# A turned context kept in device memory by the first stage that makes it and read back by three later ones

## The chip, the cores and the metric

The kernel runs on one core of one Trainium2 chip. The metric is device time of one execution in microseconds (us), lower is better. The profiler records one execution; its timeline gives the order of things, starting at 0 at the span's start.

## What is computed

A decoder of four layers works on 1024 rows of 128 numbers, `x`. A second input, the context `ctx_1024`, has 6404 rows of 128 numbers, and four of the twelve sublayers read it. Cut to those lines:

```python
# L0_xattn: a 3x3 kernel per head is made out of a projection of the whole context
x = x + _L0_xattn_ref(_layernorm(x), ctx_1024, ..., mask_SxS_bc0)
# L1_xattn and L2_xattn: 16 heads of 8 numbers, keys and values of the context
x = x + _L1_xattn_ref(_layernorm(x), ctx_1024, ctx_1024, mask_BxSxS2_if1, Wq, Wk, Wv, Wo, bo)
x = x + _L2_xattn_ref(_layernorm(x), ctx_1024, mask_BxS2_bk0, q_w, q_b, kv_w, kv_b, proj_w, proj_b)
# L3_xattn: keys and values at sampled positions between rows of the context
x = x + _L3_xattn_ref(ctx_1024, ctx_1024, _layernorm(x), mask_BxS2_if0, Wk, bk, Wv, bv, ...)
```

Each of them begins with a product of the context and weights (K = ctx Wk, V = ctx Wv, or the projection by hist_W of L0_xattn). None of them changes the context.

## The kernel before

P is 128, the context is KT = 51 tiles of 128 rows (6404 rows, padded to SP = 6528), and `k.ps` is PSUM with 8 banks of 512 numbers. TensorE sums over the partition dimension, so a product with the context needs it turned: channels on the partitions, rows of the context along the free dimension. That is the tile `ctxT`, 128 x 6528 floats.

A sublayer is a sequence of stages. A stage is a block in which each engine has its own program; semaphores order the engines within the block, and at the block's end all engines meet (in the trace this is line L68). So nothing of the next block begins before the last engine of this one is done. Within a block the order of the work on each engine is the order in which it is written; there is no planner.

`context_turned` (L1109) makes `ctxT` in a block of its own. SP loads the context by rows in four transfers (L1127, L1129), TensorE turns the 51 tiles by a product with the identity matrix (L1143), VectorE copies 13 banks of PSUM to `ctxT` (L1151). It is called four times:

- in `context_kernels` (L2512, sublayer L0_xattn). The block behind it projects `ctxT` by `hist_w` (L2565); ScalarE squares the result (L2592); meanwhile SP issues the 24 loads of `qstack` and `kstack` that the function `load_stacks` holds (passed in as `beside`, L2891). Those are used only by a much later block.
- in `masked_attention` (L1864, L1_xattn) and in `cross_attention` (L1948, L2_xattn), both times ahead of `context_sides` (L1178), the key stage. There 13 groups of 4 tiles go through a key product (L1217) and value products (L1221). ScalarE reads the key product (L1244, L1246), VectorE and GpSimd split it into three bfloat16 parts (L1264, L1271, L1297, L1299), SP stores the parts (L1311) and in three portions the values (L1319). The parts lie in three buffers: from the fourth group on, ScalarE waits for the store of three groups ago.
- in `deformable_lines` (L3952, the last sublayers), after a block that loads two bias rows (`load`, L262) and ahead of a block that copies `ctxT` to `ctxz`, two columns further right and with zeros around it (L3972 to L3977). The last block of the function makes the table of keys and values: for each tile two products (L3999), VectorE adds the bias (L4012), SP stores 256 KB (L4018), with three buffers again. At the same time ScalarE's queue issues 33 loads, of weights and small vectors, for the layers behind (L3987 to L3991).

## Time and profile before

| | us |
|---|---|
| median of 3 runs | 5533.56 |
| lowest, highest run | 5533.49, 5537.25 |
| the profiled execution, its own time | 5538.99 |
| its span in the trace | 5537.2 |

The profile's page gives busy time per engine, the span in 40 slices, the DMA queues, the chain of work that ended last, and groups of instructions by line with what ended the idle time before them. The page itself is one long average over very different stages; the stages that this change touches take some 350 us of the span, and they are read from the timeline (instructions in order of time, merged) and from windows (busy time and DMA in a stretch). Engines: PE is TensorE, PEld its weight loads, DVE VectorE, ACT ScalarE, POOL GpSimd, SP SyncE; SPq and ACTq are the DMA issues of SP and ACT. DMA queue q1 is SP's, q10 is ACT's.

### The profile page before, as it was taken

The page shows a single profiled execution, that of the slowest core. Times are in us where ns is not written, and L with a number is a line of the kernel's source. Part 1 is how long each engine was busy: PE and PEld are TensorE (multiplying, and loading weights), DVE is VectorE, ACT ScalarE, POOL GpSimd, SP SyncE. Part 2 cuts the span into 40 slices and gives each one's busy share as a digit, 9 for nine tenths or more (in the row PEclk, how much of TensorE's full clock was granted, in tenths as well). Part 3 has the DMA queues.
Part 4 walks back from the last instruction along what each step waited for, and adds up shares of the span by engine and source line. Part 5 has one row for each costly group of instructions (what it writes and reads, how often), then busy time and mean ns, then how long its engine had stood idle before and what let it go on. Part 6 is the DMA issues. An engine that isn't in the chain of part 4 may idle for free. (4 is left out here: it accounts for less than half of the span.)

```text
span 5537.2 us, 98710 instructions
## 1 busy us (share of the span) xinstructions
PE 4106.1 (74%) x37632; PEld 1563.3 (28%) x37668; DVE 3561.2 (64%) x9663; ACT 2637.9 (48%) x3507; POOL 776.1 (14%) x990
## 2 busy tenths in 40 slices
PE   4956999954799999999865999999978675601114
PEld 2333444432222222222342222222225443300002
DVE  5544666576888888888246888888843566631213
ACT  2522566651266666666413888888861011100001
POOL 0000000002000000000003000000000004777772
PEclk9967999976699999999876999999989887855567
DMA  0020000052301112111005111111110400000000
GB/s 14 1 63 16 12 12 12 5 205 76 121 22 33 33 29 82 27 28 29 8 4 166 30 43 43 45 40 40 41 17 25 154 0 8 14 13 13 13 13 8
DMA packets 144189, 216.02 MB, mean 39 GB/s; under 512 B 52385, under 2 KB 106509, under 8 KB 141971
## 3 DMA queue, kind: packets, MB, share of 16 engines
q1 hardware_dynamic: 102106, 191.29, 12.6%
q0 software_dynamic: 20480, 10.53, 1.3%
q10 hardware_dynamic: 21128, 7.88, 0.6%
q8 instruction: 298, 4.88, 0.4%
q14 instruction: 177, 1.44, 0.1%
HBM read 160.66 MB, written 48.94 MB: 38 GB/s over the span
## 5 line engine op out<-in xcount | busy, mean ns | idle before, releaser
L1764 ACT ACTIVATE probs<-ps 128x1024 f32<-128x1024 f32 x1632 | 1593.0, 1024 | 441.1 <-PE ps L1704 435.9
L1819 DVE CUSTOM_DVE_ANT_0 junk<-ps,mask 128x512 bf16<-128x512 f32 (+1 forms) x1664 | 1039.3, 668 | 125.2 <-PE ps L1658 87.2
L1720 PE MATMUL ps<-probs,vstack 128*18 128x512 f32 x6528 | 875.6, 600 | 0.0
L1658 PE MATMUL ps<-kturned,qturned 49*64 49x512 bf16 (+3 forms) x5178 | 791.0, 391 | 56.7 <-DVE maxima L1819 21.7
L1819 DVE CUSTOM_DVE_ANT_0 junk<-ps,nothing 128x512 bf16<-128x512 f32 (+1 forms) x1080 | 670.2, 657 | 131.9 <-PE ps L1658 131.5
L3464 POOL DMA_INDIRECT line<-table,index x640 | 621.1, 970 | 678.1 <-DVE index L3837 483.2
L1704 PE MATMUL ps<-qturned,kturned 53*64 53x512 bf16 x6528 | 625.8, 394 | 21.1 <-ACT probs L1764 13.6
L1658 PEld LDWEIGHTS ps<-kturned,qturned 49*64 49x64 bf16 (+1 forms) x5178 | 216.9, 103 | 876.3 <-issue 412.1
L3591 PE MATMUL ps<-ident,attended 128*128 128x128 f32 x8 | 3.8, 475 | 515.1 <-DVE attended L3861 515.1
L1689 PE MATMUL ps<-maskT,split 64*128 64x512 bf16 x1632 | 320.8, 384 | 2.6 <-DVE maxima L1819 2.5
L1704 PEld LDWEIGHTS ps<-qturned,kturned 53*64 53x64 bf16 x6528 | 186.5, 104 | 413.3 <-issue 253.6
L3844 DVE TENSOR_TENSOR prod<-line,frac 128x1280 f32<-128x1280 f32 x8 | 11.9, 1492 | 410.5 <-DMA line<-table,index 410.4
L3021 PE MATMUL ps<-plane,bands 32*32 32x512 f32 x6720 | 250.5, 610 | 25.6 <-DVE top L3176 25.6
L3120 ACT COPY powerT<-ps 128x512 f32<-128x512 f32 x280 | 164.2, 586 | 188.7 <-PE ps L3035 188.7
L1290 POOL MEMSET vall<- 128x408 f32 x4 | 3.1, 861 | 1777.9 <-POOLq L68 1777.9
L3675 ACT ACTIVATE score<-score 128x80 f32<-128x80 f32 x8 | 2.2, 269 | 518.0 <-DVE score L3854 518.0
L1819 DVE DVE_READ_ACCUMULATOR2_ANT maxima<- 128x1 f32 x2744 | 228.5, 83 | 0.0
L1815 DVE CUSTOM_DVE_ANT_0 junk<-ps,twins 128x512 bf16<-128x512 f32 x292 | 197.4, 688 | 42.1 <-PE ps L1658 32.0
L3112 ACT ACTIVATE power<-power,bias 128x512 f32<-128x512 f32 x280 | 202.0, 725 | 44.0 <-DVE bias L3184 44.0
L3166 DVE SCALAR_TENSOR_TENSOR plane<-keep,ps 128x1024 f32<-128x1024 uint8 x144 | 175.7, 1220 | 65.5 <-PE ps L3003 65.1
L3176 DVE CUSTOM_DVE_ANT_0 power<-ps,lose 128x512 f32<-128x512 f32 x280 | 176.9, 688 | 42.6 <-PE ps L3021 42.6
L1774 ACT ACTIVATE twins<-ps 128x512 f32<-128x512 f32 x292 | 171.3, 598 | 51.5 <-PE ps L1658 48.3
(736 smaller groups left out, 5342.1 us busy)
## 6 DMA issues: line engine op xcount, KB each, us to landing
vstack<-values_heads SPq DMA_DIRECT2D x128, 229.5 KB, 4.7
mask_raw<-in_mask_BxSxS_if SPq DMA_DIRECT2D x8, 3202.0 KB, 18.4
kturned<-keys_parts SPq DMA_DIRECT2D x384, 54.0 KB
kturned<-keys_parts SPq DMA_DIRECT2D x384, 48.0 KB
table<-lines SPq DMA_DIRECT2D x51, 256.0 KB, 3.4
line<-table,index POOLq DMA_INDIRECT x640, 2.3
keys_parts<-parts SPq DMA_DIRECT2D x24, 384.0 KB, 2.7
kapart<-keys_apart SPq DMA_DIRECT2D x160, 48.0 KB
```

The lines of the kernel that those rows point to most:

```text
L1658: last = nc.tensor.matmul(ring(e)[part, 0:hi - lo], qturned[rows, h % 3, m * P + part.start:m * P + part.stop], src, start=True, stop=True ...
L1689: nc.tensor.matmul(k.ps[:, 2 * (u % 2) + first, :], k.split[mine, :], maskT[mine, t, :], start=True, stop=False, skip_group_check=True)
L1704: last = nc.tensor.matmul(k.ps[to, 2 * (u % 2) + first, :], kturned[rows, h % 2, t * P + 64 * first:t * P + 64 * first + 64], qturned[rows ...
L1720: last = nc.tensor.matmul(k.ps[at:at + PAIR, 4, :], vstack[:, h % 2, first, t, :], probs[:, (h * KT + t) % slots, first, :], start=(t < 2) ...
L1764: nc.scalar.activation(probs[:, u % slots].rearrange("p b n -> p (b n)"), k.ps[:, bank:bank + 2, :].rearrange("p b n -> p (b n)"), ACT.Exp ...
L1815: nc.vector.tensor_tensor_reduce(junk[:, bank_of[e], :], ring(e), twins[:, twin[apart] % TWINS, :], 1.0, -3.0e38, ALU.add, ALU.max, maxima ...
L1819: nc.vector.tensor_tensor_reduce(junk[:, bank_of[e], 0:hi - lo], ring(e)[:, 0:hi - lo], lost, 1.0, -3.0e38, ALU.subtract, ALU.max, maxima[ ...
L3021: last = nc.tensor.matmul(k.ps[32 * j:32 * j + 32, i, :], bands[32 * i:32 * i + 32, 4 * g + j, c, :], plane[32 * i:32 * i + 32, u % 2, j, ...
L3112: nc.scalar.activation(part, part, ACT.Exp, bias=bias[:, u % 2, 1, i:i + 1], scale=1.0 / TINY).then_inc(powers, 1)
L3166: nc.vector.scalar_tensor_tensor(out=plane[:, u % 2, 2 * pair:2 * pair + 2, b * BANK + 1:(b + 1) * BANK + 1], in0=mid(keep[:, win % 2, b * ...
L3176: nc.vector.tensor_tensor_reduce(power[:, u % 2, i, b * BANK:(b + 1) * BANK], k.ps[:, i, :], lose[:, win % 2, i, b * BANK:(b + 1) * BANK], ...
L3464: nc.gpsimd.indirect_dma_start(line[:, t % 4, j, :], None, lines_of, bass.IndirectOffsetOnAxis(ap=index[:, t, j:j + 1], axis=0)).then_inc( ...
```

## The change

`context_turned` is called once, in `context_kernels`. SP stores `ctxT` to a new tensor in device memory, `k.turned_dram` (128 x 6528 floats, 3264 KB), at the start of the block behind it, ahead of the 24 loads, and waits for the store at the block's end. Both key stages begin with seven loads on ScalarE's queue, of 8 tiles each (the last of 3), and TensorE waits for a load before every second group. In `deformable_lines` three blocks fall away (the bias loads, the turning, the copy); the last block loads the bias rows and, in four pieces (4, 12, 16 and 19 tiles), the context straight into `ctxz`, ahead of those 33 loads on the same queue, and does the small fills and copies on VectorE first.

```diff
@@ context_sides
+        context_loaded = [s.sem(f"context_loaded{i}") for i in range(0, len(groups), 2)]
...
             for g, ts in enumerate(groups):
                 n = len(ts) * P
+                if g % 2 == 0:
+                    pe.wait_ge(context_loaded[g // 2], 16)
...
+            for i in range(0, len(groups), 2):
+                lo, hi = groups[i][0] * P, min((groups[i][0] + 8) * P, SP)
+                act.dma_start(ctxT[:, lo:hi], k.turned_dram[:, lo:hi]).then_inc(context_loaded[i // 2], 16)
             for g, ts in enumerate(groups):
                 n = len(ts) * P
                 act.wait_ge(key_product, g + 1)
@@ masked_attention, and the same in cross_attention
-            ctxT = context_turned(k, g)
+            ctxT = g.sb("ctxT", [P, SP])
@@ context_kernels
             ctxT = context_turned(k, g)
+            turned_stored = g.sem("turned_stored")
...
             def _(sp):
+                sp.dma_start(k.turned_dram, ctxT[:]).then_inc(turned_stored, 16)
                 beside(sp)
+                sp.wait_ge(turned_stored, 16)
@@ deformable_lines
-        load(k, [(bias[:, 0, :], row(k, n + "bk", D)), (bias[:, 1, :], row(k, n + "bv", D))])
         with Stage(nc) as f:
-            ctxT = context_turned(k, f)
-            with Stage(nc) as e:
-                done = e.sem("done")
-                block = e.block()
-
-                @block.vector
-                def _(dve):
-                    nc.vector.memset(ctxz[:, 0:2], 0.0).then_inc(done, 1)
...
-                    nc.vector.tensor_copy(ctxz[:, 2:S + 2], ctxT[:, 0:S]).then_inc(done, 1)
-        with Stage(nc) as f:
+            cuts = [0, 4 * P, 16 * P, 32 * P, S]
...
             def _(act):
                 with nc.allow_non_contiguous_dma("a few small vectors lie by partition"):
+                    act.dma_start(bias[:, 0, :], row(k, n + "bk", D)).then_inc(bias_loaded, 16)
+                    act.dma_start(bias[:, 1, :], row(k, n + "bv", D)).then_inc(bias_loaded, 16)
+                    for i in range(len(cuts) - 1):
+                        act.dma_start(ctxz[:, 2 + cuts[i]:2 + cuts[i + 1]], k.turned_dram[:, cuts[i]:cuts[i + 1]]).then_inc(context_loaded[i], 16)
                     act.dma_start(*first_mask).then_inc(loaded, 16)
...
             def _(pe):
+                pe.wait_ge(edges_ready, 5)
                 for t in range(KT):
+                    for i in range(len(cuts) - 1):
+                        if t * P == cuts[i]:
+                            pe.wait_ge(context_loaded[i], 16)
...
+                nc.vector.memset(ctxz[:, 0:2], 0.0).then_inc(edges_ready, 1)
...
+                dve.wait_ge(bias_loaded, 32)
                 for t in range(KT):
...
+                sp.wait_ge(edges_ready, 5)
@@ build
+        k.turned_dram = nc.dram_tensor("context_turned", (P, SP), F32, kind="Internal").ap()
```

How the instructions stand in a row, at the two places where queues change. SP in sublayer L0_xattn, from the context loads to the block's end (L68), of the kernel before:

```order
 L1127 DMA rows<-in_ctx 4x128
 L1129 DMA rows<-in_ctx 128x16x128 x2
 L1129 DMA rows<-in_ctx 128x18x128
 L68 UNCONDITIONAL_BRANCH
 L2554 UNCONDITIONAL_BRANCH
 L2891 DMA qstack<-parts 8x8x1152 x12
 L2891 DMA kstack<-parts 8x8x1024 x12
 L68 UNCONDITIONAL_BRANCH
```

and of the changed one:

```order
 L1127 DMA rows<-in_ctx 4x128
 L1129 DMA rows<-in_ctx 128x16x128 x2
 L1129 DMA rows<-in_ctx 128x18x128
 L68 UNCONDITIONAL_BRANCH
 L2561 UNCONDITIONAL_BRANCH
 L2563 DMA context_turned<-ctxT 128x6528
 L2900 DMA qstack<-parts 8x8x1152 x12
 L2900 DMA kstack<-parts 8x8x1024 x12
 L68 UNCONDITIONAL_BRANCH
```

The store stands ahead of the 24 loads in SP's queue. ScalarE in `deformable_lines`, from the end of the sublayer before on, in the changed kernel (before, the queue began with `mask<-in_c_one`, and the two bias loads were SP's):

```order
 L1072 ACTIVATE act_a<-ps 64x1024
 L68 UNCONDITIONAL_BRANCH
 L3982 UNCONDITIONAL_BRANCH
 L3985 DMA bias<-in_L_xattn_bk 128x128
 L3986 DMA bias<-in_L_xattn_bv 128x128
 L3988 DMA ctxz<-context_turned 128x512
 L3988 DMA ctxz<-context_turned 128x1536
 L3988 DMA ctxz<-context_turned 128x2048
 L3988 DMA ctxz<-context_turned 128x2308
 L3989 DMA mask<-in_c_one 128x1
 L3991 DMA table<-in_c_rot 128x128
 L3991 DMA within<-in_c_within 128x1024
```

Six transfers now stand ahead of the weight loads in that queue, four of them the context.

## Rows read from the trace of the kernel before

**Rows 1.** Page: busy time by engine, and the chain that ended last.

```profile
PE 4106.1 (74%) x37632; PEld 1563.3 (28%) x37668; DVE 3561.2 (64%) x9663; ACT 2637.9 (48%) x3507; POOL 776.1 (14%) x990
POOL 11%; issue 4%; DVE 3%; PE 2%; ACT 0%; DMA 0%; POOLq 0%; DVEq 0%; ACTq 0%
```

**Rows 2.** Timeline of L1_xattn, context and key stage: start, duration, instructions, idle before.

```profile
1323.87 0.17 DVE L1148 MEMSET rows<- 128x128 f32 x1 [0.38 <-PEq L68]
1324.62 5.85 SPq L1129 DMA_DIRECT2D rows<-in_ctx  x3
1330.87 6.62 PE L1143 MATMUL ps<-ident,rows 128*128 128x128 f32 x32 [13.71 <-DMA rows<-in_ctx]
1342.39 1.10 PE L1217 MATMUL ps<-ctxT,wT_L_xattn_Wk 128*128 128x512 f32 x2 [1.67 <-PEq L68]
1348.18 15.97 SPq L1311 DMA_DIRECT2D keys_parts<-parts  x6
1380.07 1.65 PE L1217 MATMUL ps<-ctxT,wT_L_xattn_Wk 128*128 128x384 f32 x2 [8.35 <-ACT parts L1246]
1403.87 8.35 PE L1920 MATMUL ps<-ident,mask 128*128 128x128 bf16 x109 [20.24 <-PEq L68]
```

**Rows 3.** Timeline of L2_xattn, the same place.

```profile
2908.88 0.17 DVE L1148 MEMSET rows<- 128x128 f32 x1 [0.38 <-PEq L68]
2928.20 1.10 PE L1217 MATMUL ps<-ctxT,wkv 128*128 128x512 f32 x2 [1.67 <-PEq L68]
```

**Rows 4.** From the views of `rows`, `keys_parts`, `table` and the integer mask: issue to landing.

```profile
DMA to landing us min/median/max: 6.2/8.8/11.4
DMA to landing us min/median/max: 2.5/2.8/11.8
DMA to landing us min/median/max: 2.0/3.4/7.4
DMA to landing us min/median/max: 12.2/18.4/25.6
```

**Rows 5.** Waits in L1_xattn from 1342 to 1372: us, times, longest.

```profile
ACT whole L1244 <- DMA keys_parts<-parts: 11.8, 5, 2.9
```

**Rows 6.** Windows: length, busy per engine, clock granted to PE, DMA share, GB/s.

```profile
1330.00:1332.00 2.00, 1.13 (x6) 1.13 (x7) 0.00 (x0) 0.00 (x0) 0.00 (x0) 0.50 1.06 294
1342.00:1344.00 2.00, 1.61 (x9) 1.16 (x10) 0.07 (x1) 0.47 (x1) 1.65 (x3) 1.00 0.00 0
1380.00:1382.00 2.00, 1.67 (x3) 0.52 (x3) 1.86 (x5) 1.98 (x5) 0.66 (x1) 0.50 0.01 5
```

**Rows 7.** Timeline of `deformable_lines`, its blocks and the block behind it.

```profile
4272.43 0.35 SPq L273 DMA_DIRECT2D bias<-in_L_xattn_bk  x1
4276.37 0.17 DVE L1148 MEMSET rows<- 128x128 f32 x1 [5.29 <-PEq L68]
4296.06 3.48 DVE L3977 COPY ctxz<-ctxT 128x6404 f32<-128x6404 f32 x1
4299.86 8.60 PE L3999 MATMUL ps<-wkv,ctxz 128*128 128x256 f32 x32 [6.52 <-PEq L68]
4384.40 2.19 DVE L3918 MEMSET state<- 128x2560 f32 x1 [6.12 <-PEq L68]
```

**Rows 8.** Windows of the table block, VectorE's line L4012 alone (two per tile).

```profile
4300.00:4350.00 50.00, 18.21 (x49) 0.84 1.00 283
4350.00:4380.00 30.00, 19.27 (x54) 0.91 0.62 239
```

**Rows 9.** Windows: the context load, the 24 loads, and a large store.

```profile
362.00:381.00 19.00, 8.42 (x51) 7.64 (x51) 8.54 (x15) 0.00 (x0) 0.00 (x0) 0.68 0.62 173
380.00:406.00 26.00, 22.28 (x102) 19.30 (x102) 19.70 (x32) 21.52 (x100) 0.00 (x0) 1.00 0.50 71
1366.00:1378.00 12.00, 5.30 (x28) 3.80 (x26) 4.44 (x8) 1.08 (x2) 4.85 (x6) 0.78 1.03 369
```

**Rows 10.** Timeline of L0_xattn: SP's issues, and the end of the block.

```profile
384.79 19.57 SPq L2891 DMA_DIRECT2D kstack<-parts  x12
407.04 0.48 DVE L2585 RECIPROCAL red<-var 128x51 f32<-128x51 f32 x1 [0.31 <-ACT var L2594]
408.02 1.28 ACT L2665 ACT_TABLE_LOAD   x1 [1.01 <-PEq L68]
```

More of the change, by code:

```diff
@@ L1967, in cross_attention @@
         with Stage(nc) as g:
-            ctxT = context_turned(k, g)
+            ctxT = g.sb("ctxT", [P, SP])
             context_sides(k, ctxT, wkv[:, 0:D], wkv[:, D:2 * D], key_bias[:], bias[:, 1, :], JOINS)
@@ L3962, in deformable_lines @@
         ctxz = g.sb("ctxz", [P, SP + P])
-        load(k, [(bias[:, 0, :], row(k, n + "bk", D)), (bias[:, 1, :], row(k, n + "bv", D))])
         with Stage(nc) as f:
-            ctxT = context_turned(k, f)
-            with Stage(nc) as e:
-                done = e.sem("done")
-                block = e.block()
-                @block.vector
-                def _(dve):
-                    nc.vector.memset(ctxz[:, 0:2], 0.0).then_inc(done, 1)
-                    nc.vector.memset(ctxz[:, S + 2:SP + P], 0.0).then_inc(done, 1)
-                    nc.vector.memset(zero[:], 0.0).then_inc(done, 1)
-                    nc.vector.tensor_copy(wkv[:, 0:D], k.wT[n + "Wk"][:]).then_inc(done, 1)
-                    nc.vector.tensor_copy(wkv[:, D:2 * D], k.wT[n + "Wv"][:]).then_inc(done, 1)
-                    nc.vector.tensor_copy(ctxz[:, 2:S + 2], ctxT[:, 0:S]).then_inc(done, 1)
-        with Stage(nc) as f:
+            cuts = [0, 4 * P, 16 * P, 32 * P, S]
+            bias_loaded = f.sem("bias_loaded")
+            context_loaded = [f.sem(f"context_loaded{i}") for i in range(len(cuts) - 1)]
+            edges_ready = f.sem("edges_ready")
             product = f.sem("product")
@@ L4005, in _ @@
                 both = bias[:].rearrange("p c (h d) -> p h c d", h=H)
+                nc.vector.memset(ctxz[:, 0:2], 0.0).then_inc(edges_ready, 1)
+                nc.vector.memset(ctxz[:, S + 2:SP + P], 0.0).then_inc(edges_ready, 1)
+                nc.vector.memset(zero[:], 0.0).then_inc(edges_ready, 1)
+                nc.vector.tensor_copy(wkv[:, 0:D], k.wT[n + "Wk"][:]).then_inc(edges_ready, 1)
+                nc.vector.tensor_copy(wkv[:, D:2 * D], k.wT[n + "Wv"][:]).then_inc(edges_ready, 1)
+                dve.wait_ge(bias_loaded, 32)
                 for t in range(KT):
```

## The prediction

> **What bounds the kernel now.** The page first: TensorE is busy 74% of the span and VectorE 64%, and the chain that ended last runs mostly through GpSimd in the last sublayers [rows 1]. Neither tells anything of this change, since these are averages over 5.5 ms, and the change touches four short places. So I read the timeline there, looking at a block's first instruction and the first of the block behind it: because all engines meet at a block's end, a block that goes away is worth the distance between the two, whoever was busy in it. In L1_xattn the turning block runs from 1323.87 to the first key product at 1342.39, 18.5 us [rows 2]; in L2_xattn from 2908.88 to 2928.20, 19.3 us [rows 3]. In the last sublayers three blocks run from 4272.43 to the first table product at 4299.86, 27.4 us [rows 7]. In all three places nothing else runs beside them, so 65.2 us stand free of cover. The waits and windows then say what the blocks behind are bound by, because the loads now run inside these.
>
> **The key stages: start of the load.** The first piece is 512 KB. No row has such a load alone. A 384 KB key store lands in 2.5 to 2.8 us from its issue, and the first 1 MB of the context rows in 6.2 us [rows 4]; between them 512 KB comes to about 3.4 us. With 0.3 us for the block's entry TensorE starts 3.7 us into the stage. The page *DMA: Bandwidth & Descriptors* of the Trainium skill (section "Anatomy of one DMA — SWDGE (gpsimd) path") gives a fixed part of about 2.0 us plus the bytes over 436 GB/s, for another path than ScalarE's. That would be 3.2 us here, and the sum below would gain 0.2 us per stage; no row here shows a 512 KB load by itself.
>
> The other pieces follow while TensorE works. The whole context takes 0.62 x 19 = 11.8 us of all 16 DMA engines when read by rows [rows 9], the mask's 3202 KB at least 12.2 us to landing [rows 4], so a piece of eight tiles comes every 1.8 us, and TensorE needs two groups' time, about 3.5 us, for one. It doesn't wait again. The seven issues are over before ScalarE has a product to read: a SP issue of a 128-row transfer takes 0.35 us [rows 7], seven some 2.5 us.
>
> **The key stages: two surcharges.** First the clock. The transposes ran at a granted clock of 0.50 (1.2 GHz) when TensorE came out of a pause, and the key stage then at 1.00 (2.4 GHz) [rows 6]. Without the transposes it is the first key products that come out of a pause. Rows 2 and 6 price one: 1.65 us for the pair of 384 columns at 0.50, against 1.10 for 512 columns, so a 512-column pair would take 2.2, 1.1 us more. TensorE gets ahead of the three-buffer loop anyway, so only the first product counts: I take 1.0 us (bounds 0 and 1.5). Second the contention. The first key store is issued 5.8 us after the first product [rows 2], so at 3.7 + 1.0 + 5.8 = 10.5 us, when the context load has about 1.8 us left. ScalarE waits for these stores, at most 2.9 us each [rows 5]. If one store takes half as long again, that is 1.0 us (bounds 0 and 2.7, a store of double length). After that the loads are over; the long part of the stage, in which values are stored at 369 GB/s [rows 9], sees none of them.
>
> So L1_xattn gives 18.5 - 3.7 - 1.0 - 1.0 = **12.8 us** (10.6 to 14.8) and L2_xattn 19.3 - 5.7 = **13.6** (11.4 to 15.6).
>
> **The table.** Here the block behind is bound by DMA itself. In its first 50 us the DMA engines are busy all the time, with SP's table stores and ScalarE's weight loads, and only 49/2 = 24.5 tiles get done; once the weights are in, 53/2 = 26.5 tiles (one of the 54 is counted in both windows) take 28.3 us, 1.07 us each [rows 8]. From there to the next block 6.1 us pass (the last store's landing, the zero rows, the meeting of the engines) [rows 7]. Bounds: if the extra 3.2 MB found room for nothing, the block would start 3.7 us in, last its 84.5 us and another 11.8 us: 27.4 - 3.7 - 11.8 = 11.9 us gained. If all of it found room, 23.7. In between: the context stands at the head of ScalarE's queue and needs 11.8 us of the engines, in which the tiles begin slowly (TensorE waits for piece 1 and comes out of a pause). I put 4 tiles by 14 us. Then a stretch like the 50 us before, 24.5 tiles; then 22.5 x 1.07 = 24.1 us; then 6.1. Together 94.2 us from 4272.4, so 4366.6 instead of 4384.4: **17.8 us** gained. What makes this better than 11.9 is that the stores done beside the context load are no longer left for the loose last part, where the DMA share is 0.62. The fills, copies and bias loads (about 1.2 us of VectorE, and two transfers issued first) lie beside the first piece's flight and cost nothing; without that cover they'd cost about 1 us. The 3.48 us copy is gone, since the load writes at the shifted place.
>
> **L0_xattn.** The store is an addition, on SP's queue. SP's issues of the 24 loads are not short: the last twelve take 19.6 us, ending at 404.4, at a DMA share of 0.50 and 71 GB/s [rows 9, 10]. SP is held until the transfers in flight have drained, so putting 3264 KB (3.34 MB) ahead moves its last issue by the store's own time. The nearest row is the value store at 369 GB/s: 9.1 us (bounds 0, if the queue takes more in, and the mask's 12.2 [rows 4]). Before, the block ended with VectorE at 407.5 [rows 10], 3.1 us after SP. So the block ends 9.1 - 3.1 = **6.0 us later** (0 to 9.1). The wait for the store itself costs nothing: it is first in the queue and has landed long before. The loads behind it are used only by a block some 80 us later.
>
> **The sum.** 12.8 + 13.6 + 17.8 - 6.0 = 38.2 us. The profiled execution took 5539.0, so 5500.8 on its terms; it lies 5.4 above the median of the runs, so 5495.4 for the median, 0.7% less. All terms at their ends give 24.8 to 54.1 us. A measurement of this kernel tells changes over about 0.2% (11 us) from none.
>
> **Rivals.**
> (a) *In the table block bytes simply add.* Its DMA share is already 1.00 for 50 us [rows 8], and the 0.62 of the rest may be what three buffers allow, not room. Then the table gives 11.9 and the time is 5495.4 + 5.9 = 5501. The page *DMA: Bandwidth & Descriptors* of the Trainium skill ("Issuing engines are not separate DMA queues") speaks for this one: transfers issued by ScalarE, SP and GpSimd run on the same 16 engines and interleave, and a second issuing engine saves only issue time. By that rule ScalarE's queue is no second road beside SP's. The trace agrees as far as 283 GB/s with both queues full, less than the 369 of one. Against the rival: the loose part gets shorter.
> (b) *The store costs nothing in L0_xattn*, because SP's queue takes the 24 loads in as before. The slow issues speak against. 5495.4 - 6.0 = 5489.
> (c) *The context loads hold up the key stores for longer*, since they are seven transfers queued at once and ScalarE waits on every store from group 3 on. If three stores each take 2.8 us more in both crosses, 5495.4 + 2 x 7.4 = 5510.
> (d) *Slower: the new tensor is written and read at the pace of `qstack` and `kstack`*, 71 GB/s [rows 9], transfers that read an internal tensor as the new ones do, and keep the DMA engines only half busy. 3.34 MB would then take 47 us each time. L0_xattn's block would end at 404.4 + 47 = 451.4, 43.9 us late. The last key product, 37.7 us into the key stage of L1_xattn, would come at 47.3, and the stage's end 23.8 us behind it at 71.1 instead of 80.0, 8.9 gained; L2_xattn, whose turning block is 0.8 longer, gains about 10. The table block would hold the weights back until 47 + 50 + 2 = 99 us, instead of 112: 13 gained. Net 12 us slower, 5546. It decides below 76 GB/s: at 44 us a transfer the four places even out, and each further us costs one in each of them. Against it: these two move 8 partitions at a time, the new ones all 128, as do the context rows, the mask and the stores, all at 250 GB/s and above.
> (e) *It doesn't do what it says*: a wait that I read as covered keeps the whole load ahead of each stage, 12.2 us instead of 3.7 in three places, and (a) with it. 5495.4 + 25.5 + 5.9 = 5527, no change to speak of.
>
> **Chances.** The forecast 0.58, (a) 0.18, (b) 0.12, (c) 0.06, (d) 0.03, (e) 0.03. All but (d) and (e) are faster by over 11 us: 0.94; within it 0.03; slower 0.03. The range takes in (a), (b) and (c), 5483 to 5510, gains of 51 to 24 us, close to all terms at their ends.
>
> **What would show it.** Right: line L1143 with 51 products, in L0_xattn only; the first key products 3.5 to 4.5 us after their stage's entry, at a granted clock of 0.50; the context landed by 13 us in each stage; the table block about 94 us long with DMA share 1.00 for some 64 us; SP's last `kstack` issue near 413 and the block behind it at 414. Wrong: long idle times of TensorE before the second to seventh pieces; waits on `keys_parts` well above 2.9 us in the first groups; a table block over 100 us; SP done before 408.

## The result, and the profile after

| | before | after |
|---|---|---|
| median of 6 runs each, on one chip | 5535.41 us | 5490.30 us |
| all runs | 5531.01 to 5541.13 | 5481.01 to 5495.32 |
| profiled execution (span) | 5539.0 (5537.2) | 5489.93 (5487.9) |

The ratio is 0.9914, with a 95% interval of 0.9904 to 0.9925: faster, by 45 us where 38.2 were forecast. The time of 5490 lies inside 5483 to 5510.

I read the four places in the traces first, because the span also drifts outside them. A place is measured from an instruction ahead of the change to the first one of the block behind it (the same two in every kernel), so an entry a little earlier than the block's own is counted with it.

| place, us (the two kernels' own traces) | before | after | gain | forecast |
|---|---|---|---|---|
| L0_xattn, first fill of `rows` to the next block | 46.2 | 51.7 | -5.6 | -6.0 |
| L1_xattn, normalising to the mask's first transpose | 97.0 | 81.1 | 15.8 | 12.8 |
| L2_xattn, its first load to the next block's | 106.3 | 90.9 | 15.4 | 13.6 |
| table, last addition to `x_sb` to the fill of `state` | 114.7 | 94.7 | 20.0 | 17.8 |
| sum | | | 45.7 | 38.2 |

The spans differ by 49.3, so 3.6 us of the gain lie where nothing was changed. Span less the four places is 5173.0 us before and 5169.4 after, and from 5158 to 5177 in the traces of the ten experiments, with no order to it: drift. L1_xattn and L2_xattn are called the two crosses below.

The page of the changed kernel answers to [rows 1], and the view of line L1143 says what is left of the transposes:

```profile
PE 4087.6 (74%) x37515; PEld 1540.9 (28%) x37515; DVE 3530.4 (64%) x9620; ACT 2637.4 (48%) x3507; POOL 774.5 (14%) x990
L1143 PE MATMUL ps<-ident,rows x51: 272/273/476, 368.1 to 377.7; 128*128 128x128 f32 x51
```

51 transposes are left, all before 378 us: the change does what it says. TensorE and VectorE together lost 49 us of work, and their shares didn't move.

**L1_xattn**, timeline, answering to [rows 2] (start, duration, engine, line, what, number, idle time before and what ended it):

```profile
1326.10 3.40 ACTq L1241 DMA_DIRECT2D ctxT<-context_turned  x7
1329.87 2.08 PE L1220 MATMUL ps<-ctxT,wT_L_xattn_Wk 128*128 128x512 f32 x2 [10.43 <-DMA ctxT<-context_turned]
1333.44 1.22 PE L1220 MATMUL ps<-ctxT,wT_L_xattn_Wk 128*128 128x512 f32 x2
1365.94 0.60 ACT L1250 ACTIVATE whole<-ps 128x512 f32<-128x512 f32 x1 [9.52 <-DMA keys_parts<-parts]
1390.31 1.97 PE L1926 MATMUL ps<-ident,mask 128*128 128x128 bf16 x17 [19.67 <-PEq L68]
```

The first product starts 3.8 us into the stage, and behind it TensorE never waits for a piece again. The first pair takes 2.08 us, the next 1.22. The windows (length, busy time of each engine, granted clock, DMA share, GB/s) show why, and how fast the context comes in:

```profile
1330.00:1332.00 2.00, 2.00 (x4) 0.97 (x5) 0.00 (x0) 0.02 (x1) 0.00 (x0) 0.50 1.01 408
1332.00:1334.00 2.00, 2.00 (x9) 1.78 (x9) 0.77 (x2) 1.06 (x2) 0.00 (x0) 0.54 1.02 418
1334.00:1336.00 2.00, 2.00 (x12) 1.45 (x11) 1.12 (x4) 1.09 (x2) 1.50 (x2) 1.00 0.96 383
```

The clock was 0.50 (1.2 GHz) until about 1334, as forecast. The rate, 408 to 418 GB/s, was not: [rows 6] show 294 for the same bytes read by rows. Next, from issue to landing, shortest, median and longest: `ctxT` (its 11.6 is the store in L0_xattn; the loads of the two crosses land within 8.0), `keys_parts`, and `ctxz` in the table block. The last line is ScalarE's waits for key stores from 1329 to 1359 (us, times, longest):

```profile
DMA to landing us min/median/max: 3.7/6.5/11.6
DMA to landing us min/median/max: 2.5/3.4/11.5
DMA to landing us min/median/max: 5.0/6.4/8.4
ACT whole L1250 <- DMA keys_parts<-parts: 11.0, 5, 2.9
```

The key stores' median is 3.4 us for 2.8 [rows 4]. That isn't the context load's doing: in other traces it is 2.9 (the changed kernel again, e9_after_again) and 2.7 (e4_warm) with the same load beside the stores, and 3.6 (e6_ahead) with no load in the key stages at all. ScalarE waited no longer for the stores, 11.0 us for 11.8 [rows 5].

**L2_xattn** [rows 3] is the same picture, 3.7 us from the block's entry to the first product:

```profile
2896.00 3.27 ACTq L1241 DMA_DIRECT2D ctxT<-context_turned  x7
2899.73 1.22 PE L1220 MATMUL ps<-ctxT,wkv 128*128 128x512 f32 x1 [5.76 <-DMA ctxT<-context_turned]
```

**The table** [rows 7], timeline:

```profile
4242.85 0.38 ACTq L3985 DMA_DIRECT2D bias<-in_L_xattn_bk  x1
4243.74 1.90 ACTq L3988 DMA_DIRECT2D ctxz<-context_turned  x4
4248.87 1.62 PE L4005 MATMUL ps<-wkv,ctxz 128*128 128x256 f32 x3 [8.84 <-DMA ctxz<-context_turned]
4334.77 2.19 DVE L3927 MEMSET state<- 128x2560 f32 x1 [6.10 <-PEq L68]
```

and windows of VectorE's line L4024 alone (two per tile; busy time and number, clock, DMA share, GB/s), answering to [rows 8]:

```profile
4243.00:4257.00 14.00, 2.26 (x6) 0.67 0.85 310
4257.00:4303.00 46.00, 17.36 (x46) 0.82 1.05 295
4303.00:4330.00 27.00, 17.76 (x50) 0.93 0.65 248
```

The block lasts 91.9 us. The first product comes 6.0 us after its entry, not 3.7; three tiles are done by 14 us, and 23 in the 46 us in which the DMA engines are full. These are full for 60 us and not for 64, and that is where the forecast's 94.2 was too long.

**L0_xattn** [rows 10], timeline:

```profile
379.60 0.36 SPq L2563 DMA_DIRECT2D context_turned<-ctxT  x1
390.02 22.13 SPq L2900 DMA_DIRECT2D kstack<-parts  x12
407.66 0.48 DVE L2594 RECIPROCAL red<-var 128x51 f32<-128x51 f32 x1 [0.31 <-ACT var L2603]
412.72 1.28 ACT L2674 ACT_TABLE_LOAD   x1 [5.10 <-PEq L68]
```

SP's last issue ends at 412.15 (forecast 413), and the next block starts at 412.7 (forecast 414). VectorE was done at 408.1, so SP now ends the block. Counted from the place's start, SP's last issue moved 8.7 us, where 9.1 was forecast.

### The profile page after: what moved, and what is told of

Read it like the earlier page. It is cut to its first block and busy times, and to the rows that moved or that the text cites. A ratio compares the mean times of both kernels' runs of the same rounds, so it can differ in the third digit from the quotient of the medians.

```text
span 5487.9 us, 98350 instructions
## 1 busy us (share of the span) xinstructions
PE 4087.6 (74%) x37515; PEld 1540.9 (28%) x37515; DVE 3530.4 (64%) x9620; ACT 2637.4 (48%) x3507; POOL 774.5 (14%) x990
## 3 DMA queue, kind: packets, MB, share of 16 engines
q1 hardware_dynamic: 96994, 184.66, 12.2%
## 5 line engine op out<-in xcount | busy, mean ns | idle before, releaser
L1664 PE MATMUL ps<-kturned,qturned 49*64 49x512 bf16 (+3 forms) x5178 | 790.7, 391 | 57.1 <-DVE maxima L1825 21.7
L1710 PE MATMUL ps<-qturned,kturned 53*64 53x512 bf16 x6528 | 625.2, 394 | 21.0 <-ACT probs L1770 13.6
L3853 DVE TENSOR_TENSOR prod<-line,frac 128x1280 f32<-128x1280 f32 x8 | 11.9, 1492 | 407.7 <-DMA line<-table,index 407.7
L3030 PE MATMUL ps<-plane,bands 32*32 32x512 f32 x6720 | 250.4, 609 | 25.6 <-DVE top L3185 25.5
```

The source lines that it names most:

```text
L1664: last = nc.tensor.matmul(ring(e)[part, 0:hi - lo], qturned[rows, h % 3, m * P + part.start:m * P + part.stop], src, start=True, stop=True ...
L1710: last = nc.tensor.matmul(k.ps[to, 2 * (u % 2) + first, :], kturned[rows, h % 2, t * P + 64 * first:t * P + 64 * first + 64], qturned[rows ...
L3030: last = nc.tensor.matmul(k.ps[32 * j:32 * j + 32, i, :], bands[32 * i:32 * i + 32, 4 * g + j, c, :], plane[32 * i:32 * i + 32, u % 2, j, ...
```

## The experiments

All times of places are measured as in the table above. In this table "to first" is from the place's start to the first product of TensorE, "behind" from there to the place's end. `before` and `after` are the two kernels' own traces.

| kernel | L0 | L1: to first + behind | L2: to first + behind | table: to first + behind |
|---|---|---|---|---|
| before | 46.2 | 35.5 + 61.5 | 41.1 + 65.3 | 30.2 + 84.5 |
| after | 51.7 | 20.7 + 60.4 | 25.7 + 65.3 | 8.8 + 85.9 |
| e1_store_only | 54.4 | 35.7 + 60.0 | 41.7 + 65.8 | 30.6 + 84.4 |
| e2_loads_later | 46.1 | 20.9 + 62.1 | 25.8 + 65.8 | 8.7 + 86.4 |
| e3_bias_behind | 52.7 | 20.9 + 60.7 | 25.5 + 66.3 | 5.7 + 89.2 |
| e4_warm | 52.0 | 21.1 + 60.1 | 27.6 + 66.4 | 8.8 + 83.8 |
| e5_double | 53.0 | 20.6 + 60.7 | 25.6 + 66.2 | 8.8 + 91.9 |
| e6_ahead | 52.0 | 17.0 + 60.7 | 28.4 + 65.0 | 8.8 + 86.6 |
| e7_all | 49.0 | 17.1 + 60.2 | 28.8 + 64.7 | 5.6 + 90.6 |
| e8_aimed | 47.9 | 17.1 + 61.2 | 21.7 + 64.7 | 8.7 + 86.6 |
| e9_after_again | 53.4 | 20.8 + 60.2 | 25.8 + 65.8 | 8.7 + 85.9 |
| e10_short_rows | 55.0 | 21.4 + 63.5 | 25.9 + 69.2 | 8.4 + 89.6 |

Where two kernels are alike in a place, the parts to the first product repeat within 1 us. The rest repeats less well: L0_xattn is 51.7 to 54.4 in seven traces that are alike there, and the part behind the first product is 60.2 to 62.1 in L1_xattn (eight traces) and 83.8 to 86.6 in the table (six). Single executions of the changed kernel lie up to 15 us apart. So places are compared here, with that spread of up to 3 us in mind, and whole times only where a kernel ran several times.

### The store alone

The kernel before, with the new tensor and the store, and nothing that reads it:

```diff
             def _(sp):
+                sp.dma_start(k.turned_dram, ctxT[:]).then_inc(turned_stored, 16)
                 beside(sp)
+                sp.wait_ge(turned_stored, 16)
```

> The kernel before with the store of the turned context added and nobody reading it. Read in the trace: from the fill of the row tile (L1148) in L0_xattn to the first instruction of the block behind the projection, 46.2 us before, 51.7 after. Theory (SP is held until its queue has drained, so the store's 9 us move SP's last issue past the end of VectorE's work): 51.5 to 52. Rival (the 5.6 us come from something else in the changed kernel, as TensorE's clock or where the tensors lie): 46 to 47. The other three places stay as before: 81.6, 85.6 and 114.7 us.

5542.41 us, one execution, beside 5543.18 of the kernel before. L0_xattn took 54.4 us, 8.2 more than before and longer than the 52 of the theory:

```profile
376.30 0.36 SPq L2557 DMA_DIRECT2D context_turned<-ctxT  x1
386.24 25.07 SPq L2894 DMA_DIRECT2D kstack<-parts  x12
405.72 0.48 DVE L2588 RECIPROCAL red<-var 128x51 f32<-128x51 f32 x1 [0.31 <-ACT var L2597]
411.86 1.28 ACT L2668 ACT_TABLE_LOAD   x1 [6.17 <-PEq L68]
```

SP ends the block here too, 5.1 us behind VectorE. Rival (b), a free store, is out. Over the seven traces with this store ahead of the 24 loads the place is 51.7 to 54.4 us long, 5.6 to 8.2 more than before. An eighth, e10_short_rows, writes the tensor in rows of 512 bytes: there the store lands after 13.5 us instead of 10.8 to 11.9, and the place is 55.0.

### The 24 loads moved one block back

```diff
             def _(sp):
                 sp.dma_start(k.turned_dram, ctxT[:]).then_inc(turned_stored, 16)
-                beside(sp)
                 sp.wait_ge(turned_stored, 16)
...
+            @block.sync
+            def _(sp):
+                beside(sp)
```

The second part stands in the block behind. 

> The changed kernel with the 24 loads of qstack and kstack moved into the block behind, whose SP has nothing else; the store stays where it is. Theory: the block is as short as before, 46.2 us (VectorE ends it again, the store of 9 us is covered), and the 24 loads are covered in the block behind, which stays at its 83 us. So 5.5 us come back: about 5485 us. Rival (the store or its wait is itself the cost): the block stays at 51 to 52 us.

5484.83 us (one execution), and L0_xattn at 46.1, all of the 5.6 us back:

```profile
380.62 0.36 SPq L2563 DMA_DIRECT2D context_turned<-ctxT  x1
407.04 0.48 DVE L2593 RECIPROCAL red<-var 128x51 f32<-128x51 f32 x1 [0.31 <-ACT var L2602]
408.02 1.28 ACT L2677 ACT_TABLE_LOAD   x1 [1.01 <-PEq L68]
412.22 22.93 SPq L2903 DMA_DIRECT2D kstack<-parts  x12
```

The store and its wait stay in the block and cost nothing. What cost 5.6 us was SP, held by issues of loads that stand behind the store. In the block behind, which is 83.6 us long in this trace as in the kernel before and in the changed one, they are covered: the last ends at 435, the block at 491.6.

### The bias loads behind the first piece

```diff
-                    act.dma_start(bias[:, 0, :], row(k, n + "bk", D)).then_inc(bias_loaded, 16)
-                    act.dma_start(bias[:, 1, :], row(k, n + "bv", D)).then_inc(bias_loaded, 16)
                     for i in range(len(cuts) - 1):
                         act.dma_start(ctxz[:, 2 + cuts[i]:2 + cuts[i + 1]], k.turned_dram[:, cuts[i]:cuts[i + 1]]).then_inc(context_loaded[i], 16)
+                        if i == 0:
+                            act.dma_start(bias[:, 0, :], row(k, n + "bk", D)).then_inc(bias_loaded, 16)
+                            act.dma_start(bias[:, 1, :], row(k, n + "bv", D)).then_inc(bias_loaded, 16)
```

> The changed kernel with the two bias loads of the table block behind the first context piece in ScalarE's queue. In the changed kernel TensorE begins 6.0 us into that block instead of the 3.7 forecast, and the DMA rate was under 100 GB/s until the bias rows were through. Theory: the broadcast bias loads hold the first piece; now TensorE begins at about 4 us. As the block is bound by DMA for its first 60 us, its length (91.9 us) falls by 0 to 2. Rival (the piece is slow by itself, as its target begins 8 bytes off): TensorE still begins at 6 us.

5480.69 us (one execution).

```profile
4240.26 0.33 ACTq L3986 DMA_DIRECT2D ctxz<-context_turned  x1
4243.20 5.25 PE L4006 MATMUL ps<-wkv,ctxz 128*128 128x256 f32 x16 [5.75 <-DMA ctxz<-context_turned]
4247.38 2.08 DVE L4025 TENSOR_TENSOR lines<-ps,bias 128x256 f32<-128x256 f32 x6 [5.96 <-DMA bias<-in_L_xattn_bv]
4332.37 2.19 DVE L3927 MEMSET state<- 128x2560 f32 x1 [6.07 <-PEq L68]
```

The first product came 2.9 us after the first issue, for 6.0 in the changed kernel, so two loads of 64 KB each, spread over all partitions, had held a piece of 256 KB for 3.1 us. The rival, a piece that is slow by itself, is out. The place stayed at 94.9 us, but this says little of what a late start costs. VectorE adds the bias to every product, and here it waited for the bias: its first addition came 7.1 us after the first issue, for 8.2 in the changed kernel:

```profile
4251.03 0.75 DVE L4024 TENSOR_TENSOR lines<-ps,bias 128x256 f32<-128x256 f32 x2 [7.03 <-PE ps L4005]
```

So of the 3.1 us only 1.1 reached the additions and the stores behind them, and 1.1 us can't be told from the spread of the table. Whether a block with full DMA engines hides a late start isn't shown by this run.

### TensorE warmed up while the first piece is in flight

```diff
         def _(pe):
+            for _ in range(36):
+                nc.tensor.matmul(k.ps[:, 7, 0:P], k.ident16[:], k.ident16[:], start=True, stop=True)
             for g, ts in enumerate(groups):
```

> The changed kernel with 36 idle products (bfloat16, 128 columns, into a PSUM bank that nothing reads) ahead of TensorE's first wait in both key stages. The first key products then find a granted clock of 1.00 and take 1.1 instead of 2.1 us. Theory A (the clock surcharge reaches the stage's end, as forecast): each cross's stage gets 1.0 us shorter, 65.7 to 64.7 and 70.0 to 69.0. Theory B (from group 3 on the stage waits for stores and then for DMA as a whole, which absorbs a late start of a microsecond or two): no change in length beyond 0.4 us.

5491.36 us (one execution); L1_xattn 81.1 as in the changed kernel, L2_xattn 94.0, 3.1 longer. Neither cross got shorter, and L2_xattn lies outside both theories, but the two tell different things. In L1_xattn the warming worked: the clock reached its full level sooner (windows of this kernel),

```profile
1330.00:1332.00 2.00, 2.00 (x22) 2.00 (x21) 0.00 (x0) 0.00 (x0) 1.83 (x3) 0.50 0.88 301
1332.00:1334.00 2.00, 1.92 (x11) 1.17 (x10) 0.00 (x0) 0.03 (x1) 0.00 (x0) 0.77 1.02 416
```

and the last value store was issued 46.8 us after the first product, where it is 47.8 in the changed kernel. So the slow clock does cost 1.0 us up to that store. It was not seen in the total because the first product started 0.4 later and the last store took 0.7 longer to the stage's end (13.3 us for 12.6; over all traces 12.4 to 14.2, more than the 1.0 that is looked for). In L2_xattn the piece landed only 5.9 us after the entry, the warming products had been over for 3 us, and the first pair ran at 0.50 again:

```profile
2898.35 4.99 ACTq L1243 DMA_DIRECT2D ctxT<-context_turned  x7
2898.39 2.88 PE L1215 MATMUL ps<-ident 128*128 128x128 bf16 x36 [2.07 <-PEq L68]
2904.25 2.08 PE L1222 MATMUL ps<-ctxT,wkv 128*128 128x512 f32 x2 [2.98 <-DMA ctxT<-context_turned]
```

Why the piece came 2 us later there isn't settled. The seven issues took 4.99 us for 3.27, but the load as a whole wasn't late: 293 GB/s came in on mean until the first product (233 in the changed kernel), and the last piece landed 8.1 us after its issue, for 7.8. It was the first piece that finished late. As a remedy the warming is worth nothing here.

### The context loaded twice in the table block

ScalarE loads the same four pieces once more, into a tile that nothing reads, right behind the first four.

```diff
+                    for i in range(len(cuts) - 1):
+                        act.dma_start(spare[:, cuts[i]:cuts[i + 1]], k.turned_dram[:, cuts[i]:cuts[i + 1]]).then_inc(spare_loaded, 16)
                     act.dma_start(*first_mask).then_inc(loaded, 16)
```

> The changed kernel with the whole context loaded a second time in the table block, into a tile that nobody reads, right behind the four pieces and ahead of the weight loads. Read: the block's length from ScalarE's first issue to the first fill of the last block, 91.9 us. Forecast's model (stores go on beside the load and shorten the loose part): 11.8 us of DMA work costs 5.9, so 98. Rival (a) (bytes add): 103.7. A third (there is slack for all of it): 92 to 94.

5502.07 us (one execution, 5539.29 before). The place took 100.7 us, 6.0 more, from its first issue to the fill of `state` 97.9. Windows (busy time of each engine, clock, DMA share, GB/s) of its first 68 us:

```profile
4253.00:4267.00 14.00, 8.13 (x28) 6.57 (x28) 3.02 (x10) 0.00 (x0) 0.00 (x0) 0.66 0.86 320
4267.00:4321.00 54.00, 35.23 (x100) 24.08 (x100) 18.89 (x50) 0.16 (x1) 0.00 (x0) 0.78 1.05 318
```

That is the figure that the forecast's model gave (98) and half of rival (a)'s 11.8. But the agreement is partly luck. For the same four loads, ScalarE's queue shows 43.0% of 115 us for 36.7% (view of the queues, 4230 to 4345), 7.2 us of all 16 engines, not the 11.8 that both the model and rival (a) used. So 6.0 of some 7 us reached the end (5.3 to 8.1 against the spread of the other traces): the bytes add nearly in full, as rival (a) had it, at a price that is over a third lower. Half of them, 3.6, lies outside that. The first context load gives about the same: the block grew from 84.5 us behind its first product to 91.9 in all, 7.4.

### The context loads issued earlier

In both crosses SP issues the seven loads in the normalising block, one sublayer step ahead.

```diff
+            if ahead is not None:
+                ahead(sp)
...
+            ctxT, context_loaded, ahead = context_ahead(k, c)
+            normalise(k, loads=[(bo[:], row(k, "L1_xattn_bo", D))], ahead=ahead)
```

> The changed kernel with the seven context loads of both crosses issued by SP in the sublayer's first block (the normalisation), some 20 us ahead of the key stage, so that neither their flight nor their contention lies in it. TensorE begins 0.2 us into the key stage, at a granted clock of 0.50 in L1_xattn. Theory (the 3.8 us of flight stand on the path; contention is small and absorbed): each of the two places gets 3.5 to 4.5 us shorter, 65.7 to about 61.8 and 70.0 to about 66. Rival (contention had cost 2 us or more at the end as well): 6 us or more shorter each. Third (the DMA-bound part absorbs the flight too): under 2 us.

5478.43 us (one execution). L1_xattn gave 3.4 us, its start of the load. TensorE came out of a pause there with the load long over, so this cross also shows the slow clock alone: the first pair took 2.05 us at 0.50, and the last value store was issued 47.8 us after the first product, as in the changed kernel. L2_xattn lost 2.5, and the trace names the cause, small loads behind the big ones in SP's queue:

```profile
2866.26 3.75 SPq L1188 DMA_DIRECT2D ctxT<-context_turned  x7
2870.80 0.31 SPq L1404 DMA_DIRECT2D lost<-in_mask_BxS_bk  x1
2878.34 0.28 DVE L1397 SCALAR_TENSOR_TENSOR ends<-lost,ends 51x128 bf16<-51x128 uint8 x1 [7.72 <-DMA lost<-in_mask_BxS_bk]
```

### The three edits together

The loads of the first stage moved back, the biases behind the first piece, and the context loads as in e6_ahead. 

> The changed kernel with the three edits together: the 24 loads in the block behind, the bias loads behind the first piece, the crosses' loads ahead. If the gains of the single edits add (5.5 + 1 + 2 x 4), about 14 us less than the changed kernel: 5476 us by the median, ratio to the kernel before 0.989. If they don't (a covered transfer collides elsewhere), 5482 to 5490.

5485.29 us median of five runs (5480.71 to 5492.80); ratio to the kernel before 0.9905, interval 0.9891 to 0.9918. The gains didn't add: 14 us were hoped for, and the four places together are 316 us for 318.4 in the changed kernel. L1_xattn kept its gain (77.3), L2_xattn repeated its loss (93.5), the table took 96.2, and L0_xattn came to 49.0 with VectorE itself done only at 48.5.

### Aimed at each place, beside the changed kernel

As e7_all, but with the biases left where they were and the second cross's loads issued by SP in the block that projects the queries, behind all small loads. The changed kernel ran again beside it.

```diff
-                     (key_bias[:], dr["L2_xattn_kv_b"][0:D].rearrange("(p a) -> p a", a=1))], ahead=ahead)
+                     (key_bias[:], dr["L2_xattn_kv_b"][0:D].rearrange("(p a) -> p a", a=1))])
...
-            project(k, k.hT, NT, wq[:], D, q, bias[:, 0, :])
+            project(k, k.hT, NT, wq[:], D, q, bias[:, 0, :], ahead=ahead)
```

> The changed kernel with three edits: the 24 loads of the first stage behind the store go to the block behind; the seven context loads of the first cross are issued by SP in its normalising block, as in e6_ahead; those of the second cross are issued by SP in the block that projects the queries, some 6 us ahead of the key stage and behind all of end_row's and soft_ends' small loads. Theory (each wait was on the path in its own stretch, and in e6_ahead the second cross lost its 3.5 us to the small mask loads that queued behind the context): against the changed kernel the first stage 5.5 us shorter (46.1 where 51.7), the first cross 3.4 shorter (77.7 where 81.1), the second cross 3.0 to 3.8 shorter (87.1 to 87.9 where 90.9), its first product less than 1 us behind the block's entry; the table as in the changed kernel (94.7). Sum 12 us less than the changed kernel. Rival (the second cross's loss in e6_ahead came from the loads themselves, wherever they are issued, since they share the DMA engines with what the block behind loads and stores): the second cross at 90 to 93.5, sum 7 to 9 us less.

> The changed kernel itself, unchanged, beside e8_aimed on the same chip. Both theories: the stretches as in the first profile, first stage 51.7, first cross 81.1, second cross 90.9, table 94.7, each within 1 us; the ratio to the kernel before 0.990 to 0.9925. It shows how far the time between the stretches drifts from one execution to the next, and e8_aimed is read against it: 12 us less by the theory, 7 to 9 by the rival.

e8_aimed 5480.26 us median (5465.64 to 5486.93; ratio to before 0.9891, interval 0.9876 to 0.9906); the changed kernel 5492.13 (5480.39 to 5495.36; 0.9913, 0.9900 to 0.9927). Timeline of e8_aimed:

```profile
2884.57 0.28 DVE L1402 SCALAR_TENSOR_TENSOR ends<-lost,ends 51x128 bf16<-51x128 uint8 x1 [2.05 <-DMA lost<-in_mask_BxS_bk]
2891.44 3.53 SPq L1193 DMA_DIRECT2D ctxT<-context_turned  x7
2897.31 1.10 PE L1238 MATMUL ps<-ctxT,wkv 128*128 128x512 f32 x2 [2.07 <-PEq L68]
```

The mask load is waited for 2.05 us instead of 7.72, and the first pair takes 1.10 us, at full clock from its start. Against e9_after_again the places give 5.4 + 2.7 + 5.2 - 0.7 = 12.6 us, the medians 11.9: the theory's 12. Part of it is spread. e9_after_again is the changed kernel, and its L0_xattn took 53.4, not the 51.7 within 1 us that was expected; against the first trace of the changed kernel the sum is 10.5. What is clear of the spread is L2_xattn: 86.4, where the rival had 90 to 93.5. The two intervals overlap a little (0.9900 to 0.9906), so the whole times alone don't settle it. This version has the lowest ratio of those that ran several times, though its interval overlaps that of e7_all too.

### The same tensor with short rows

The changed kernel with `context_turned` laid out tile by tile, so that the loads stay and the contiguous rows shrink, from 1.5 KB and more (4 KB in most loads) to 512 bytes. Two things change with it that the cut doesn't show: the store writes short rows as well, and the table's last piece takes 62 KB of padding along, 2% of the bytes.

```diff
-        k.turned_dram = nc.dram_tensor("context_turned", (P, SP), F32, kind="Internal").ap()
+        k.turned_dram = nc.dram_tensor("context_turned", (KT, P, P), F32, kind="Internal").ap().rearrange("t p n -> p t n")
...
-                act.dma_start(ctxT[:, lo:hi], k.turned_dram[:, lo:hi]).then_inc(context_loaded[i // 2], 16)
+                act.dma_start(ctxT[:, lo:hi].rearrange("p (t n) -> p t n", n=P), k.turned_dram[:, lo // P:hi // P, :]).then_inc(context_loaded[i // 2], 16)
```

> The changed kernel, but the new tensor is laid out tile by tile (51 x 128 x 128) instead of by partition (128 x 6528): the same bytes, loads and cuts, each contiguous row 512 bytes long as in the original context, instead of 2 KB to 9 KB. Theory (the length of the row sets the rate, and the table block pays in bytes): the context loads run at 285 to 305 GB/s where the changed kernel shows 408 to 418, so all seven need 11 to 12 us; the table 3 to 5 us longer, 97.5 to 99.5 for 94.7; the first key product 0.3 to 0.8 us later, the crosses else as before, 81 to 83 and 91 to 93, since TensorE needs 3.5 us for a piece. Rival (the slow rate of before came from the input tensor or from another queue, not from the row): 400 GB/s and more as in the changed kernel, the table 94.2 to 95.2.

5510.72 us (one execution, 5548.79 before). A window, the issues in L1_xattn, and ScalarE's queue from 1333 to 1349 (packets, MB, share):

```profile
1339.00:1341.00 2.00, 2.00 (x9) 1.56 (x8) 0.00 (x0) 0.00 (x0) 0.00 (x0) 0.50 1.16 290
1333.23 9.46 ACTq L1241 DMA_DIRECT2D ctxT<-context_turned  x7
q10 hardware_dynamic: 6640, 3.34, 81.6%
```

290 GB/s, as from the original rows: the length of the row sets the rate, and the rival is out. The table took 98.0 us, 3.3 longer, inside the theory's band, and ScalarE's queue took 39.3% of 115 us there, for 36.7 and 36.1% in the two traces of the changed kernel: 3.0 to 3.7 us more of all engines. The crosses fell outside it, 84.9 for 81 to 83 and 95.1 for 91 to 93. No piece was late. The seven issues took ScalarE 9.46 us for 3.40, and since it issues them itself, it read its first product 5.2 us after that product's start, where it is 2.1 in the changed kernel; these 3.1 us lasted to the last value store (50.6 for 47.8 behind the first product in L1_xattn, 56.7 for 53.3 in L2_xattn). The prediction had put issues at 0.35 us each and off the path. That was right only because the rows are long.

## Why the prediction was right, point by point

- **The start of the load** (3.7 us into the stage): measured 3.8 and 3.7. All of it is flight (3.7 us from issue to landing, for the 3.4 of the rows); the 0.3 us for the block's entry were not there, since ScalarE's first issue stands at the block's start. e6_ahead in L1_xattn and e8_aimed in L2_xattn show it was on the path: issued ahead, the first product comes 3.6 and 4.0 us sooner. The rule in the Trainium skill (*DMA: Bandwidth & Descriptors*, "Anatomy of one DMA — SWDGE (gpsimd) path"), which is stated for another path, gives an estimate of 3.2 us for the flight; the 3.7 measured here is nearer to the rows' 3.4.
- **The clock surcharge** (1.0 us per cross): the step was right. In L1_xattn it is 46.6 us from the first product to the last value store in e1_store_only, 46.8 in e4_warm (full clock sooner), and 47.8 both in the changed kernel and in e6_ahead (slow clock, no load beside it): 1.0 to 1.2. In L2_xattn it is 52.6 before and 53.3 after, 0.7. That this lasts to the stage's end isn't shown, since the rest of the stage varies by more.
- **The contention** (1.0 us per cross): this step failed, the term was put at 1.0 us and the runs show 0.2 or less in L1_xattn. e6_ahead has no load in the key stage of L1_xattn and comes to the last value store at the same 47.8 us as the changed kernel; e4_warm, which has the load and little of the slow clock, is 0.2 us over e1_store_only. In L2_xattn e8_aimed, with the load still coming in at 421 GB/s but a fast clock, needs 52.3 us; e7_all and e6_ahead, with the load long over, need 52.3 and 52.7.
- **The gain in L1_xattn** was 15.8 for 12.8. One us is the contention that wasn't there. The rest comes from the trace of before. There a store of the values, `vall`, in this place landed after 13.6 us, the longest of all,

```profile
DMA to landing us min/median/max: 9.7/12.0/13.6
```

and ScalarE's next read of a product came 36.5 us after the first product. In e1_store_only, with the same key stage, that store took 12.2 us and the read came at 34.9. Read against e1_store_only, L1_xattn gave 95.6 - 81.1 = 14.5. I had priced everything from one execution, and that one had a long store in this place. In L2_xattn 15.4 came for 13.6: the 1.0 of contention again, 0.3 of the clock, and the rest because the stage ended 12.0 us behind its last value store, 12.6 before, which is within its spread.
- **The table** (17.8): measured 20.0. Several sizes were off, some against each other. The cover for the bias loads didn't hold: the first product came at 6.0 us, not 3.7 (e3_bias_behind). What that cost at the block's end isn't shown. And the load itself was priced at 11.8 us of all engines, from the context read 512 bytes at a row, near 290 GB/s [rows 6, 9]; with long rows it ran at 408 to 418 and took 7 to 8 us. e10_short_rows shows that the row is the reason, for 3.0 to 3.7 of the 4 to 5 us between. The idea that half of the bytes find room was wrong: e5_double lost 6.0 of 7.2. The price was too high and the share that reaches the end too low, the two nearly cancel, and the block ended 2.3 us below the forecast's 94.2. So the size of this term is partly luck.
- **L0_xattn** (-6.0, SP's last issue near 413): measured -5.6, 412.2. e1_store_only and e2_loads_later show the mechanism from both sides. That the size met so well is partly luck: over seven traces the cost is 5.6 to 8.2 us, and the store, put at 9.1, landed after 10.8 to 11.9.
- **The rivals**: (b) fell with e1_store_only; (c) needed three key stores to take 2.8 us longer each, and the waits for them didn't grow; (d), which would have decided below 76 GB/s, met 408; (e) fell with the 51 transposes and the 3.8 us. (a) was right that bytes add and wrong in their price, 11.8 for some 7 us. Its sum with 7.2 still gives 3.7 + 84.5 + 7.2 = 95.4 us for the block where 91.9 were measured: it puts the flight of the first piece on top of the bytes, while the DMA engines are already 0.85 busy in the first 14 us.
- **The issues** (0.35 us each, 2.5 for seven): measured 3.4, and 9.5 with short rows. With long rows they were off the path, as said.
- **What stays open**: why the first piece came 2 us later in the second cross of e4_warm, what a late start costs in the table block, and the drift outside the four places.

## What to carry to other kernels

A block that nothing covers is worth its whole length when it goes, less the flight of what replaces it; that flight can then be moved ahead too, but only to a place in the queue where no small load that someone waits for stands behind it. Where a block's DMA engines are full, count the bytes that are added, nearly in full, and price these, and the issues, from transfers with rows as long as the new ones. A loop that waits for two inputs starts with the later one: putting one load ahead of the other wins only the difference. An added transfer must also be read in the queue of the engine that issues it: here the store was free, and the loads queued behind it were not. And a single trace gives a term no better than it repeats, here within 1 us in one part and 3 in another.

## What was not expected of the hardware

- The same 3.34 MB came in at 408 to 418 GB/s with rows of mostly 4 KB, and at 290 with rows of 512 bytes, both with the DMA engines full. ScalarE's queue in the changed kernel, 1326 to 1340 (packets, MB, share of 14 us, so 8.9 us of all engines), stands against 6640 packets and 81.6% of 16 us (13.1) in e10_short_rows:

```profile
q10 hardware_dynamic: 1008, 3.34, 63.4%
```

  The Trainium skill (*DMA: Bandwidth & Descriptors*, "Specifications") puts the shortest transfer for line rate at 512 bytes; here rows of that length stayed 30% below the long ones.
- With short rows an issue also takes its engine longer, 9.46 us for seven instead of 3.40.
- Two 64 KB loads that spread one row over all partitions, at the head of a queue, held a 256 KB load behind them for 3.1 us. A small load behind seven large ones was waited for 7.72 us instead of 2.05 (e6_ahead, e8_aimed).
- A store of 3.34 MB ahead of 24 loads moved SP's last issue 8.7 to 11.4 us later (seven traces), though the store itself landed 10.8 to 11.9 us after its issue, long before them (windows of the changed kernel, columns as above):

```profile
379.00:386.00 7.00, 4.45 (x13) 3.69 (x14) 3.42 (x8) 0.95 (x5) 0.00 (x0) 0.76 0.84 353
393.00:400.00 7.00, 7.00 (x34) 6.15 (x33) 5.62 (x9) 7.00 (x33) 0.00 (x0) 1.00 0.53 72
```
